# Time-mixing block with two-part half-precision weights: weights laid out by the host, low parts from a diagonal held in TensorE, and a shorter preparing block

## The reference

```python
x = x + attn(layernorm(x)); x = x + ffn(layernorm(x))
# attn: xx = shift(x) - x;  xk, xv, xr, xg = x + xx * time_maa_{k,v,r,g}
r, k, v = xr @ Wr.T, xk @ Wk.T, xv @ Wv.T      # 32 heads of 16, chunks of Q = 64 tokens
g = silu(xg @ Wg.T)
att = rc @ kc * w_mat                           # per chunk and head, decay powers and a bonus diagonal
yc = att @ vc + rc @ state * wb
state = ws * state + kc * wk @ vc
out = (groupnorm(y) * gamma + beta) * g @ Wo.T
# ffn: gelu(X @ W0.T + bias0) @ W1.T + bias1, 512 -> 2048 -> 512, activations rounded to float16
```

## Time and profile before

| what | value |
|---|---|
| median of 3 runs | 2046.94 us |
| the profiled execution's own time | 2050.78 us |
| its span, first to last instruction | 2049.0 us |
| TensorE busy | 1999.8 us, 98% |
| VectorE, ScalarE, GpSimdE busy | 85%, 63%, 15% |
| mean granted TensorE clock | 0.993 |
| chain that ended last | TensorE 81% |
| DMA | 385.42 MB, mean 188 GB/s |

### The profile page before, as it was taken

How to read it: one execution, slowest core, us unless ns; L and a number is a source line. 1 busy time by engine, 2 the same in 40 slices (tenths; PEclk the granted TensorE clock), 3 DMA queues, 4 the chain that set the end, 5 groups by cost and what they waited for, 6 DMA issues and landing times.

```text
span 2049.0 us, 64453 instructions
## 1 busy us (share of the span) xinstructions
PE 1999.8 (98%) x27206; PEld 1424.3 (70%) x27206; DVE 1738.7 (85%) x3687; ACT 1293.0 (63%) x2081; POOL 317.5 (15%) x329
## 2 busy tenths in 40 slices
PE   5889999999999999999999999999999999999999
PEld 4767667777666777766777766667776677777676
DVE  7778889888888888888988888888888898888771
ACT  7775566676555677656667656667765666766452
POOL 1011111111111111111111111111111111111110
PEclk8999999999999999999999999999999999999999
DMA  6776666777666677766667766667777666776656
GB/s 217 161 193 194 177 178 182 199 197 196 177 194 171 189 198 195 185 190 189 173 194 202 199 174 186 181 181 202 192 195 184 191 180 185 199 202 177 181 175 191
DMA packets 403216, 385.42 MB, mean 188 GB/s; under 512 B 256880, under 2 KB 304112, under 8 KB 402928
## 3 DMA queue, kind: packets, MB, share of 16 engines
q1 hardware_dynamic: 401296, 381.12, 68.1%
q10 hardware_dynamic: 1632, 0.18, 0.1%
HBM read 232.32 MB, written 22.54 MB: 124 GB/s over the span
## 4 chain that ended last, share of the span: by engine, by line
PE 81%; SPq 4%; DVE 4%; ACT 4%; DMA 3%; issue 2%; POOL 0%; ACTq 0%; DVEq 0%
PE F L1149 19%; PE F L1086 16%; PE B L892 9%; PE B L1053 8%; PE sc L892 7%; PE YT L924 6%; PE YT L892 3%; DMA y<-ygT 3%; PE YT L976 3%; SPq L2044 2%; PE sc L954 2%; PE YT L995 2%; PE YT L1086 1%; PE F L847 1%; PE YT L1025 1%
## 5 line engine op out<-in xcount | busy, mean ns | idle before, releaser
L1149 PE MATMUL F<-ring,hT 128*128 128x512 f16 x1984 | 467.7, 379 | 0.5 <-issue 0.5
L1149 PEld LDWEIGHTS F<-ring,hT 128*128 128x128 f16 x1984 | 189.1, 98 | 198.4 <-issue 0.8
L1086 PE MATMUL F<-xT,kept 128*128 128x256 f16 x2400 | 276.8, 273 | 2.0 <-issue 1.2
L892 PE MATMUL B<-mix,WT 128*128 128x256 f16 x2304 | 267.5, 273 | 0.0
L1785 ACT ACTIVATE hT<-F,b,f_rho 128x256 f16<-128x256 f32 x480 | 243.4, 560 | 37.8 <-PE F L1086 37.7
L1086 PEld LDWEIGHTS F<-xT,kept 128*128 128x128 f16 x2400 | 234.6, 98 | 42.1 <-issue 2.6
L892 PEld LDWEIGHTS B<-mix,WT 128*128 128x128 f16 x2304 | 222.7, 98 | 33.3 <-DVE gT L1389 0.3
L279 DVE SCALAR_TENSOR_TENSOR mixf<-dx,maa,xnT 128x256 f32<-128x256 f32 x512 | 238.7, 527 | 0.1
L1742 ACT ACTIVATE Shl<-S 128x256 f16<-128x256 f32 x128 | 53.1, 415 | 236.2 <-PE YT L995 125.8
L1988 POOL TENSOR_TENSOR Shl<-S,Shl 128x256 f16<-128x256 f32 x128 | 89.2, 697 | 708.5 <-ACT Shl L1742 702.1
L1736 ACT ACTIVATE att<-att 128x512 f16<-128x512 f32 x256 | 147.5, 624 | 67.7 <-DVE att L1350 67.7
(11 more groups left out here) (208 smaller groups left out, 3108.6 us busy)
## 6 DMA issues: line engine op xcount, KB each, us to landing
ring<-w_dram SPq DMA_DIRECT2D x352, 512.0 KB, 3.7
kx<-kT SPq DMA_DIRECT2D x96, 256.0 KB, 3.8
rx<-rT SPq DMA_DIRECT2D x96, 256.0 KB, 4.5
xa<-in_L_attn_x SPq DMA_DIRECT2D x32, 512.0 KB, 5.0
vbd<-vN SPq DMA_DIRECT2D x256, 64.0 KB, 2.1
x<-in_L_attn_x SPq DMA_DIRECT2D x32, 512.0 KB, 5.0
out<-x SPq DMA_DIRECT2D x31, 512.0 KB, 3.5
kept<-in_L_ffn_W SPq DMA_DIRECT2D x5, 512.0 KB, 12.0
```

The source lines that it names most:

```text
L892: mm = eng.matmul(out[:, gg * BT:(gg + 1) * BT], WT[:, w, a, kk, rows(g)], mix[:, m % 2, b, kk, :], start=(i == 0 and kk == 0), stop=(i == ...
L1086: mm = eng.matmul(up_place(f, j)[:, i * BT:(i + 1) * BT], w, xT[:, :, kk, :], start=(kk == 0 and a == 0), stop=(kk == G - 1 and a == 1))
L1149: mm = eng.matmul(F[:, t, :], hT[:, k, rows(t)], ring[:, use % RING, i, a * C:(a + 1) * C], start=(k == 0 and a == 0), stop=(k == NH - 1 a ...
```

## The change

**By the host** (`laid_out`): all weights but Wv come with input channels on the partitions, each partition's row contiguous (8 KB for an attention matrix, 4 KB for a piece); the row order that six DMAs gathered for Wk and Wr is made there. The mixing factors, gamma, beta and bias0 come as one array of 40 columns (`cols`) instead of seven transfers of four-byte elements.

**Preparing block**: no transposes of weights; high and low parts of K and R are made straight from the loaded rows. V keeps its product with the centring matrix, but its parts, and those of G and O, are made in the main block (`act_late_hi`, `dve_late_lo`): V at the start of step 0, G in its middle, O's high part near its end and O's low part after it. All table exponentials stand ahead of the first square. V, G and O have one common scale computation. The raw V, G and O lie in buffers that the attention uses later. GpSimdE's clearing of buffers moves into the block.

**Pieces**: TensorE holds the diagonal (then -1 on the diagonal) and the piece moves, 512 columns at a time; the raw pieces lie in `ring` instead of `kept`; high parts of the first five are written in their place; no DMA transposes; each part is stored as soon as it is there.

The diff, cut to what is spoken of:

```diff
 
-    def parts_of(q):
-
-        return place_of(q)[:, 0:2 * C], place_of(q)[:, 2 * C:4 * C]
+    def low_place(q):
+
+        return kept[:, q, 1, :] if q < KEPT else place_of(q)[:, 0:2 * C]
 
...
-        if n == 0:
-            source = W0[2 * P * j:2 * P * (j + 1), :]
-        else:
-            if j >= KEPT:
-                eng.wait_ge(s_stash[j], 32)
-            source = W1[:, 2 * P * j:2 * P * (j + 1)]
-        if n == 0:
-            eng.dma_start(raw_piece(PIECES * n + j).rearrange("p (b c) -> p b c", b=2),
-                          source.rearrange("(b p) c -> p b c", p=P)).then_inc(s_raw[j], 16)
-        else:
-            for i in range(2):
-                eng.dma_start(raw_piece(PIECES * n + j)[:, C * i:C * i + C].rearrange("p (b c) -> p b c", b=G),
-                              source[:, P * i:P * i + P].rearrange("(b p) c -> p b c", p=P)).then_inc(s_raw[j], 16)
-
-    def act_piece_square(eng, n, j, squares):
+        if n:
+            if j < KEPT:
+                eng.wait_ge(s_plo, j + 1)
+            else:
...
+    def w_hi(eng, u, half, src):
+
+        eng.activation(WT[:, u, 0, 2 * half:2 * half + 2, :], src, ACT.Identity, scale=scl[:, u:u + 1]).then_inc(s_hi, 1)
+
+    def half_of(raw, half):
+
+        return raw[:, 2 * C * half:2 * C * half + 2 * C].rearrange("p (k e) -> p k e", k=2)
+
+    def late_half(u, half):
+
+        if u == V_:
+            return Y if half else F[:, :, :]
+        return half_of(raw_late[u], half)
+
+    def act_late_hi(eng, u, half):
+        if u == V_:
+            eng.wait_ge(s_vc, half + 1)
+        w_hi(eng, u, half, late_half(u, half))
+
+    def dve_late_lo(eng, u, half):
+        eng.wait_ge(s_hi, 2 * ORDER.index(u) + half + 1)
+        dve_weight_lo(eng, u, half, late_half(u, half))
...
-            return 16 * (G + 2) if u in (K_, R_) else 16
+        def raw_of(u):
+            return raw[u][:, :] if u in (K_, R_) else raw_late[u]
 
         def load(eng, u):
 
-            if u in (K_, R_):
-                source = weights[u].rearrange("(b q e) c -> b e q c", b=G, q=4)
-                for b in range(G):
-                    if b < 2:
-                        eng.dma_start(raw[:, u, b, :], source[b]).then_inc(landed[u], 16)
-                    else:
-                        for p in range(2):
-                            at = rows_of(b, p)
-                            eng.dma_start(raw[at, u, b, :], source[b][N * p:N * p + N]).then_inc(landed[u], 16)
+            if u == V_:
+                eng.dma_start(raw_of(u).rearrange("p (b c) -> p b c", b=G),
+                              weights[u].rearrange("(b p) c -> p b c", p=P)).then_inc(landed[u], 16)
             else:
-                eng.dma_start(raw[:, u, :, :], weights[u].rearrange("(b p) c -> p b c", p=P)).then_inc(landed[u], 16)
+                eng.dma_start(raw_of(u), weights[u]).then_inc(landed[u], 16)
 
         def act_square(eng, u):
...
                 act_square(eng, R_)
                 act_mix_hi(eng, 0, 0)
                 act_square(eng, V_)
+                act_fades(eng)
                 for half in range(2):
                     act_hi(eng, R_, half)
                 act_square(eng, G_)
-                act_hi(eng, V_, 0)
+                act_mix_hi(eng, 0, 1)
                 act_square(eng, O_)
-                act_hi(eng, V_, 1)
-                act_exps(eng, 1)
-                act_fades(eng)
-                for half in range(2):
-                    act_hi(eng, G_, half)
-                act_mix_hi(eng, 0, 1)
-                for half in range(2):
-                    act_hi(eng, O_, half)
 
             @block.gpsimd
             def _(eng):
-                eng.memset(means[:, :], 1.0 / P).then_inc(s_means, 1)
+                eng.memset(mean_of[:, :], 1.0 / P).then_inc(s_ones, 1)
+                eng.memset(S[:, :], 0.0).then_inc(s_zero, 1)
+                eng.memset(Shl[:, 0, :, :].rearrange("p a c -> p (a c)").bitcast(F32), 0.0).then_inc(s_zero, 1)
+                for t in (kx, rx):
+                    eng.memset(t[:, :, :, :].rearrange("p q g t -> p (q g t)").bitcast(F32), 0.0)
+                eng.memset(vbd[:, :, :, :, :, :].rearrange("p t c a b d -> p (t c a b d)").bitcast(F32), 0.0).then_inc(s_zero, 1)
 
             @block.vector
...
                 eng.memset(xnT[:, :, 0:1], 0.0).then_inc(s_carry, 1)
+                dve_scale(eng, K_)
                 dve_exponents(eng)
-                dve_scale(eng, K_)
                 dve_tables(eng, 0)
-                eng.wait_ge(s_maa, 64)
+                eng.wait_ge(s_maa, 16)
                 dve_dx(eng, 0)
                 for g in range(G):
                     dve_mix(eng, 0, 0, g)
@@ -700,16 +687,10 @@
                 for g in range(G):
                     dve_mix(eng, 0, 1, g)
                 mix_lo(eng, 0, 0)
-                dve_scale(eng, V_)
                 for half in range(2):
                     dve_lo(eng, R_, half)
-                dve_lo(eng, V_, 0)
-                dve_scale(eng, G_)
-                dve_lo(eng, V_, 1)
-                dve_scale(eng, O_)
-                for half in range(2):
-                    dve_lo(eng, G_, half)
                 dve_tables_rest(eng)
+                dve_scale(eng, V_)
         own.close()
 
     prepare()
...
         else:
-            eng.wait_ge(s_wlo, 10)
+            eng.wait_ge(s_wlo, 6)
         for i in range(2):
-            for b in range(G):
-                at = C * i + P * b
-                eng.matmul(F[:, i, rows(b)], raw_piece(q)[:, at:at + P], diagonals[k % DIAGONALS],
-                           start=(b == 0), stop=False)
-            for b in range(G):
-                at = C * i + P * b
-                mm = eng.matmul(F[:, i, rows(b)], high(q)[:, at:at + P], minus_one[:, :],
-                                start=False, stop=(b == G - 1))
+            at = slice(C * i, C * i + C)
+            eng.matmul(F[:, i, :], diagonals[k % DIAGONALS], raw_piece(q)[:, at], start=True, stop=False)
+            mm = eng.matmul(F[:, i, :], minus_one, high(q)[:, at], start=False, stop=True)
         mm.then_inc(s_ptr, 1)
 
...
-            eng.dma_start(wd[q].rearrange("p (k a c) -> p a k c", k=2, a=2)[:, a],
-                          parts_of(q)[a].rearrange("p (k c) -> p k c", k=2)).then_inc(s_stash[j], 16)
+    def sp_store(eng, q, part):
+
+        if part == 0:
+            eng.wait_ge(s_phi, q + 1)
+            done = s_hst[q % 2]
+        else:
+            eng.wait_ge(s_plo, q + 1)
+            done = s_stash[q % PIECES]
+        eng.dma_start(wd[q].rearrange("p (k a c) -> p a k c", k=2, a=2)[:, part],
+                      (low_place(q) if part else high(q)).rearrange("p (k c) -> p k c", k=2)).then_inc(done, 16)
 
...
         if n <= nb + 1:
             if n == 0:
                 mix_lo(eng, 0, 1)
+                for half in range(2):
+                    dve_late_lo(eng, V_, half)
             if early:
                 mixing(G)
-            if n == 0:
-                dve_weight_lo(eng, O_, 0, Y)
             if ahead:
                 dve_stats(eng, n + 1, 0)
             mixing(1)
...
                 dve_factors(eng)
+                for half in range(2):
+                    dve_late_lo(eng, G_, half)
             if tail and n != 1:
                 for t in range(NT):
                     dve_normalized(eng, n - 1, t)
@@ -1660,6 +1619,9 @@
                 dve_variance(eng, n, 0)
             dve_state(eng, n, 3)
             dve_take_y(eng, n, 1)
+        if n == 0:
+            for half in range(2):
+                dve_late_lo(eng, O_, half)
         if tail:
             dve_residual(eng, n - 1, 1)
...
         if n == 0:
-            for j in range(4):
-                act_piece_square(eng, 0, j, squares)
+            for half in range(2):
+                act_late_hi(eng, V_, half)
+            act_minus_one(eng)
+            for j in range(2):
+                act_piece_square(eng, 0, j)
         if att_n:
             act_K_hi(eng, n, 0)
         if n == 0:
-            act_minus_one(eng)
-            act_piece_square(eng, 0, 4, squares)
+            for j in range(2, 5):
+                act_piece_square(eng, 0, j)
         if n == 1:
             act_K_hi(eng, n, 1)
         if n == 2:
@@ -1872,20 +1835,22 @@
         if att_n and n != 1:
             act_K_hi(eng, n, 1)
         if n == 0:
-            act_piece_square(eng, 0, 5, squares)
-            act_piece_square(eng, 0, 6, squares)
+            for half in range(2):
+                act_late_hi(eng, G_, half)
+            act_piece_square(eng, 0, 5)
+            act_piece_square(eng, 0, 6)
         if n == 1:
-            act_piece_square(eng, 1, 5, squares)
+            act_piece_square(eng, 1, 5)
         if ff and not att_n:
             act_fnorm(eng, n - 2)
...
             if n == 0:
-                act_piece_square(eng, 1, 3, squares)
+                for half in range(2):
+                    act_late_hi(eng, O_, half)
```

(40 more changed lines are left out.)

290 lines of the change are left out of this document (119 added, 171 removed).

## The result

Predicted 2044.2 us (2038.5 to 2049.0). Measured **2054.32 us**, median of 10 runs, against 2048.65 us for the kernel before beside it: ratio 1.0032, 95% interval 1.0022 to 1.0042. The change makes the kernel 0.3% slower. One of the ten runs took 2118.66 us at a granted clock of 0.933 and is left out of the ratio. The profiled execution took 2058.37 us, span 2056.5.

The account below looks back on a forecast made before the run. TensorE was taken as the bound, full from 200 us on, so only the start could move: -3.5 (step 0 earlier) - 1.8 (low parts) + 2.6 (Wo) = -2.7 us, from 2046.94 to 2044.2 us, range 2038.5 to 2049.

Parts of the forecast that it names:

- Preparing block: Before step 0: exponentials from about 8.9 us, block end at 34.6 instead of 42.75, step 0 starting 8.0 us earlier.
- Square to scale: In the preparing block: from Wk's square to VectorE's first scale step 2.7 us, as before, so 15.2.
- the third rival: Start: tables wait behind Wk's and Wr's long runs; exponentials from 11.6 cancel the gain, bound 8.2 us gives 2052.0; chance 0.15.
- my nearest row: Start of exponentials: the trace's last table landing at 7.8 us, near which the delay was taken as +0.4 us.
- Mean on the pieces: Step 0: TensorE has the mean over the feed-forward pieces at 52.6 us instead of 56.78, then idles 4 us.
- First low part: Step 0, TensorE: first low part of a piece 3.5 us earlier than the old 62.38; sign: at 58 to 60.
- Low parts: TensorE's pieces, steps 0 and 1: 2.15 us each instead of 2.30, 0.13 taken as saved, 1.8 us in all.
- Wo: End of step 0: Wo's low part on VectorE stands ahead of step 1's mixes and costs 2.6 us (0 to 2.6).
- First rival: Step 1: the slow V product falls under cover, the second runs at full clock; -5.4 us, 2041.5; chance 0.25.
- second rival: Tables 1 us earlier, no slow product at the mean, first rival holds too; about -7.5 us, 2039.5; chance 0.12.
- Everything after 200 us alike, moved by the same amount: Sign for the steady steps: the profile after 200 us is unchanged except for one common shift.

Follow-up runs that it names:

- a1: The changed kernel with the stores of W1's first two high parts issued earlier by SyncE; 2049.06 us, 0.9992 of the kernel before.
- a2: The changed kernel with the high part of W1's third piece in a buffer of its own (vw32); 2048.97 us, 0.9998 of the kernel before.
- c1: The changed kernel itself, run and traced once more; 2052.80 us, 1.0017 of the kernel before.
- g1: The changed kernel itself, unedited, run again for a third profile; no median or ratio of its own is given.
- g2: The changed kernel itself, unedited, run again for one more profile; no median or ratio of its own is given.
- c4: The changed kernel with those stores earlier, Wk's load behind the small tables and Wo's parts in gaps of step 0; 2044.32 us, 0.9969 of the kernel before.
- e2: The same kernel as c4, measured again for an interval from more runs; 2042.00 us, 0.9963 of the kernel before.

## Why the prediction was wrong

**The step that failed** is the sentence "The 16 DMA transposes that go were waited for by nobody in the chain: worth nothing there, and the stores that replace them have a piece's time to land." The transposes were worth nothing, but they had also set when a buffer of high parts came free, with three buffers in turn, so that W1's third piece found one free. Now there are two, and a buffer is free when its store has landed. In step 0 that holds. In step 1 the store stands behind vbd and two loads in SyncE's queue: 6.1 us from ready to issued, 5.4 to landed, and ScalarE waits from 127.8 to 134.6. I had counted what the store needs, and not the queue that it stands in. Priced by a1: 4.9 us at the landmark, against the mean of four traces, of which 2.3 are TensorE's longer wait (4.27 by the mean, against 1.95) and 2.6 the low clock behind it. The first part is sure. The second hangs on the clock: a2, also without the stop, kept slow products and gained 2.5.

The other terms, by their order:

- Preparing block. Square to scale 2.7 predicted, 17.89 - 15.17 = 2.7 measured; from there to the block's end 19.0 predicted, 19.1 measured. But the exponentials started at 11.34, not 8.9: the third rival, "the loads bite", came true with 2.8 of its 8.2 us, near its point of no gain (11.6). My argument against it, that the tables were issued ahead of Wk, was wrong for the one that counts: in the changed kernel Wk is issued at 1.26 us and `un` at 1.68, where before it was Wk at 1.75. The Trainium skill's rule (DMA: Bandwidth & Descriptors, "Queues, rings and completion order") had been a better guide to the direction than my nearest row: by it the term was to lie nearer the upper bound than 0.4. It measured 2.8, counted from the old 8.49, still well below the bound of 8.
- Mean on the pieces: 54.05 against 52.6, TensorE idle 4.03 ahead of it as said, the V product slow as said (4.44). First low part 60.16, 1.3 later than forecast.
- Low parts: 2.15 predicted, and the f32 pair of 512 columns is 1.02 to 1.10 for two records with 0.22 behind; over the first two pieces the gain grew by 0.3 as forecast (third piece at 69.92 instead of 72.42), then by 1.8 because the third was slow in the earlier trace rows and not here, then by another 0.3 over the last five instead of 0.65.
- Wo: 2.6 predicted. From step 1's K product to the mixes the gain fell from 4.6 to 1.6: 3.0, a little over the upper bound.
- First rival: it came true in two of four traces. In the first (and in c1) the first V product of step 1 was slow under cover (4.32) and the second at full clock: the gain at its end was 4.3 against 5.4 in the forecast of that rival. In g1 and g2 both products were slow (4.45 us for the first, 4.44 and 4.43 for the second).
- Baseline. A single execution stood for the kernel before. Its landmark is 2.1 us later than the mean of four, and a gain measured from it counts a slow piece that half of the executions do not have.
- Arithmetic. The second rival's terms add up to -7.3, not -7.5, and two scale chains of 1.05 are 2.1, not 2.2; nothing hangs on either.

"Everything after 200 us alike, moved by the same amount" failed too. By the means of four traces each the changed kernel is 3.1 us later at the landmark and takes 3.9 us more behind it; the store alone is enough for the first (4.9 us by a1), the second is not explained.

With the three faults mended (c4, e2) the time is 2044.3 and 2042.0 us, about what I had predicted for the change as it is. That is no credit: I had named the start as a rival, priced Wo nearly right, and not seen the store at all.

## What to carry to other kernels

When a buffer's release moves from one transfer to another, follow the new transfer through its queue: who issues it, what stands ahead there, and which engine will wait in order behind it. Load small tables that gate the first chain ahead of large loads, or split these loads and issue them later. Before a gain of some us is counted from one trace, look at more of them, for pieces whose clock differs.

## What the runs showed of the hardware

- Two gaps of the same length in front of TensorE's pieces behave differently: after 1.95 us idle the pieces of a1 run at full clock, after 1.90 those of a2 are slow from the third piece's second half on; after 2.27 us at step 0 two executions of the kernel before are at full clock and two at half. The length of the gap alone does not tell.
- A store of 256 KB from SBUF to DRAM landed 5.4 us after its issue, in a stretch in which the DMA engines are busy for 0.48 of the time; by the median such stores took 2.8 to 4.1 us in the same trace.
- A 16 KB table that ScalarE's queue issues at 1.68 us lands at 10.7 us beside Wk and Wr in rows of 8 KB, at 8.6 when Wk comes in four transfers of 2 KB rows and Wr is issued 2.7 us later, and at 7.1 when neither is issued before it has landed.
- Products added into a wait can keep the clock up: with 2.8 us of repeated G products the piece behind them ran at full clock, and the landmark came 1.2 us before the mean, not later; the time shows no gain.
